# A group-normed convolution and a five-step matching pursuit on one core: the hand-written order of work of all engines is replaced by another

## The reference

```python
x = x + conv3x3_circular(_gn(x), L0_conv_weight)          # 64 -> 64 channels
x = x + pursuit(_gn(x), L1_conv_dictionary)

def pursuit(z, dictionary):        # patches of 64 x 4 x 4 = 1024 numbers, 16384 in all
    D = dictionary / norm          # (1024, 512)
    h_bar = (D.T @ X).T; h = h_bar; G = D.T @ D + 1e-5 * I
    for k in range(1, 6):
        index = argmax(|h| where not yet chosen)
        L = cholesky row from G[I, index];  x_stack = solve with L, h_bar[I]
        h = h_bar - x_stack @ G[I]
    return D @ coeffs
```

## Time and profile before

| what | value |
|---|---|
| device time, median of 3 runs | 3638.73 us (3585.6 to 3663.25) |
| profiled execution | 3610.05 us, its span 3608.2 us |
| mean granted TensorE clock | 0.916 |
| busy: PE, DVE, ACT, POOL | 85%, 71%, 65%, 53% |
| bytes moved by DMA | 428.38 MB, 119 GB/s |
| the chain that ended last | PE 51%, issue 11%, POOL 11%, ACT 11%, DVE 9%, DMA 5% |

### The profile page before, as it was taken

How to read it: one execution, slowest core, us unless ns; L and a number is a source line. 1 busy time by engine, 2 the same in 40 slices (tenths; PEclk the granted TensorE clock), 3 DMA queues, 4 the chain that set the end, 5 groups by cost and what they waited for, 6 DMA issues and landing times.

```text
span 3608.2 us, 35041 instructions
## 1 busy us (share of the span) xinstructions
PE 3072.9 (85%) x9488; PEld 1309.0 (36%) x9488; DVE 2577.4 (71%) x6596; ACT 2361.3 (65%) x3795; POOL 1915.2 (53%) x1861
## 2 busy tenths in 40 slices
PE   6796979889898999989898998989898998985446
PEld 2232334333333434333343433433343433332123
DVE  2027877768787787778777786878778786878871
ACT  3436676667867676667767676776767666665444
POOL 0015565555556565655556565665556566565651
PEclk8998989999999999989999999999999999998768
DMA  3424343533545253444535354344525443342222
GB/s 113 152 88 135 112 146 74 165 92 129 150 130 152 70 189 90 143 120 131 151 93 168 83 170 104 132 132 143 145 72 182 96 157 99 107 113 59 57 61 47
DMA packets 131028, 428.38 MB, mean 119 GB/s; under 512 B 55696, under 2 KB 55952, under 8 KB 106128
## 3 DMA queue, kind: packets, MB, share of 16 engines
q0 software_dynamic: 91136, 202.10, 23.7%
q1 hardware_dynamic: 39696, 224.05, 17.1%
HBM read 289.70 MB, written 136.31 MB: 118 GB/s over the span
## 4 chain that ended last, share of the span: by engine, by line
PE 51%; issue 11%; POOL 11%; ACT 11%; DVE 9%; DMA 5%; ACTq 0%; POOLq 0%; DVEq 0%
PE gen_ps L917 18%; PE gen_ps L908 17%; PE conv_ps L951 10%; POOL v L478 9%; PE conv_ps L958 4%; DMA u<-marked_rows,chosen 3%; ACT hot L542 3%; DVE u L831 2%; ACT score L616 2%; DVE idx L731 2%; DVE top L722 2%; POOL u L490 1%; DVE h L839 1%; ACT rb L554 1%; ACT hot L545 1%
## 5 line engine op out<-in xcount | busy, mean ns | idle before, releaser
L478 POOL DMA_INDIRECT v<-gram_rows,cell x1280 | 1288.4, 1007 | 1009.2 <-DVE cell L740 467.4
L908 PE MATMUL gen_ps<-ct,dt 128*128 128x512 f32 x2048 | 959.1, 624 | 54.3 <-ACT rb L554 36.3
L917 PE MATMUL gen_ps<-dn,z 128*128 128x512 f32 x2048 | 920.6, 603 | 45.9 <-ACT h L577 23.1
L490 POOL DMA_INDIRECT u<-marked_rows,chosen x504 | 552.3, 1096 | 511.3 <-DVE chosen L736 216.4
L951 PE MATMUL conv_ps<-xh,wc 128*128 128x512 f32 x1536 | 727.7, 625 | 76.1 <-ACT xa L584 75.1
L616 ACT ACTIVATE score<-h 128x512 f32<-128x512 f32 x640 | 380.0, 605 | 383.1 <-DVE h L839 250.1
L908 PEld LDWEIGHTS gen_ps<-ct,dt 128*128 128x128 f32 x2048 | 400.8, 200 | 568.9 <-issue 546.7
L917 PEld LDWEIGHTS gen_ps<-dn,z 128*128 128x128 f32 x2048 | 388.2, 193 | 535.3 <-issue 497.2
L722 DVE MAX8 top<-score 128x8 f32<-128x512 f32 x640 | 417.2, 690 | 212.0 <-ACT score L616 197.0
L831 DVE SCALAR_TENSOR_TENSOR u<-u,nl 128x512 f32<-128x512 f32 x748 | 515.6, 748 | 72.7 <-DMA u<-marked_rows,chosen 69.7
L951 PEld LDWEIGHTS conv_ps<-xh,wc 128*128 128x128 f32 x1536 | 301.8, 200 | 470.5 <-issue 469.3
(11 more groups left out here) (103 smaller groups left out, 1860.2 us busy)
## 6 DMA issues: line engine op xcount, KB each, us to landing
xh<-x_paired SPq DMA_DIRECT2D x128, 650.0 KB, 4.0
xa<-x_pairs SPq DMA_DIRECT2D x64, 1024.0 KB, 6.8
y_rows<-xa SPq DMA_DIRECT2D x64, 1024.0 KB, 5.1
y_rows<-rb POOLq DMA_DIRECT2D x64, 1024.0 KB, 8.5
v<-gram_rows,cell POOLq DMA_INDIRECT x1280, 2.4
u<-marked_rows,chosen POOLq DMA_INDIRECT x504, 3.9
...
```

Source lines behind the costliest of these rows:

```text
L478: pool.indirect_dma_start(v[:, g, k - 1, j, t:t + 1], None, cells, bass.IndirectOffsetOnAxis(ap=cell[:, g, k // (KMAX - 1), j, t:t + 1], a ...
L490: pool.indirect_dma_start(kept(img, g, k, t), None, marked, bass.IndirectOffsetOnAxis(ap=chosen[:, g, t:t + 1], axis=0))\
L908: last = pe.matmul(to[:], dt_[:, a, d, :], ct[:, a, :], start=(a == 0), stop=(a == NA - 1))
L917: last = pe.matmul(to[:], z[:, t % 2, d // PATCH, d % PATCH, :], dn[:, d, :], start=(d == 0), stop=(d == ND - 1))
```

## The change

No instruction is added, removed or resized. Another table stands in each of the plans (`VECTOR_PLAN`, `SCALAR_PLAN`, `ADD_PLAN`, `BANKS`, and the tail's vector, scalar and add plans), and PE's calls in `period` and `tail` stand in another order. In the changed file lines are one higher in this part (L616 becomes L617).

Of the diff, one or two lines of each plan, the new `BANKS`, and PE's period from convolve 1 on:

```diff
...
 VECTOR_PLAN = {
-    1.5: [("co", 0)], 5: [("ce", 0, 0)], 8.5: [("ce", 0, 1)], 23.5: [("co", 1), ("ce", 1, 0)], 29.5: [("gn", 1, 1)],
+    1.5: [("co", 0)], 3: [("ce", 0, 0)], 10.5: [("ce", 0, 1)], 23.5: [("co", 1)], 24: [("ce", 1, 0)],
+    30: [("ce", 1, 1), ("gn", 1, 1)], 31: [("gn", 1, 2), ("gn", 1, 3)], 37: [("gn", 0, 1)],
...
 SCALAR_PLAN = {
-    39: [("re", 1, 7), ("rt", 0), ("h", 2), ("h", 3)],
...
+    0: [("z", 4), ("oh", 0, 0, 1)],
+    37: [("h", 2), ("re", 1, 6)], 39: [("rt", 0), ("h", 3), ("re", 1, 7)],
...
 ADD_PLAN = {
-    4: [(0, 0)], 6: [(0, 1)], 7: [(1, 0)], 8: [(1, 1)],
+    4: [(0, 0)], 5: [(0, 1)], 7: [(1, 0)], 9: [(1, 1)],
 }
...
 BANKS = (
-    (("corr", 4), ("corr", 7), ("re", 0, 2), ("re", 0, 5), ("re", 1, 0), ("re", 1, 3), ("re", 1, 5), ("re", 1, 7)),
-    (("corr", 5), ("re", 0, 0), ("re", 0, 3), ("re", 0, 6), ("re", 1, 1), ("corr", 0), ("corr", 1), ("corr", 2)),
-    (("corr", 6), ("re", 0, 1), ("re", 0, 4), ("re", 0, 7), ("re", 1, 2), ("re", 1, 4), ("re", 1, 6), ("corr", 3)),
+    (("corr", 4), ("corr", 7), ("re", 0, 2), ("re", 0, 5), ("re", 1, 0), ("corr", 0), ("re", 1, 4), ("re", 1, 6)),
+    (("corr", 5), ("re", 0, 0), ("re", 0, 3), ("re", 0, 6), ("re", 1, 1), ("re", 1, 3), ("re", 1, 5), ("corr", 3)),
+    (("corr", 6), ("re", 0, 1), ("re", 0, 4), ("re", 0, 7), ("re", 1, 2), ("corr", 1), ("corr", 2), ("re", 1, 7)),
 )
...
                     convolve(i, 1)
                 if p:
                     turn(i - 2, 0, 0)
+                if own:
+                    convolve(i, 2)
+                if p:
+                    turn(i - 2, 0, 1)
+                if own:
+                    convolve(i, 3)
                 if b:
                     correlate(i, 1, 5)
-                if p:
-                    turn(i - 2, 0, 1)
-                if own:
-                    convolve(i, 2)
-                    convolve(i, 3)
+                if own:
+                    convolve(i, 4)
                 if b:
                     correlate(i, 1, 6)
                 if p:
                     turn(i - 2, 0, 2)
                 if own:
-                    convolve(i, 4)
+                    convolve(i, 5)
                 if p:
                     turn(i - 2, 0, 3)
                 if b:
...
                 if p:
                     recon(i, 2, 0, 0)
                     recon(i, 2, 0, 1)
-                    recon(i, 2, 0, 2)
-                if own:
-                    convolve(i, 5)
-                if p:
-                    recon(i, 2, 0, 3)
                 if own:
                     convolve(i, 6)
                 if p:
+                    recon(i, 2, 0, 2)
+                    recon(i, 2, 0, 3)
                     recon(i, 2, 0, 4)
+                if own:
+                    convolve(i, 7)
+                if p:
                     recon(i, 2, 0, 5)
                     recon(i, 2, 0, 6)
-                if own:
-                    convolve(i, 7)
-                if p:
+                    recon(i, 2, 0, 7)
                     turn(i - 2, 1, 0)
-                    recon(i, 2, 0, 7)
+                    turn(i - 2, 1, 1)
                 if own:
                     average(i, 1)
-                if p:
-                    turn(i - 2, 1, 1)
-                if own:
-                    spread(i, 1)
                 if p:
                     turn(i - 2, 1, 2)
                     turn(i - 2, 1, 3)
+                if own:
+                    spread(i, 1)
+                if p:
                     recon(i, 2, 1, 0)
                     recon(i, 2, 1, 1)
                     recon(i, 2, 1, 2)
+                if own:
+                    correlate(i, 0, 0)
+                if here[-1]:
+                    average(i + 1, 0)
+                if p:
                     recon(i, 2, 1, 3)
                 if own:
-                    correlate(i, 0, 0)
+                    correlate(i, 0, 1)
                 if p:
                     recon(i, 2, 1, 4)
                     recon(i, 2, 1, 5)
                 if own:
-                    correlate(i, 0, 1)
-                if here[-1]:
-                    average(i + 1, 0)
+                    correlate(i, 0, 2)
                 if p:
                     recon(i, 2, 1, 6)
                 if here[-1]:
                     spread(i + 1, 0)
+                if own:
+                    correlate(i, 0, 3)
                 if p:
                     recon(i, 2, 1, 7)
-                if own:
-                    correlate(i, 0, 2)
                 if here[-1]:
                     bias(i + 1, 1 - par)
-                if own:
-                    correlate(i, 0, 3)
...
```

26 lines of the change are left out of this document (12 added, 14 removed), and 107 rows, old and new, of tables (SCALAR_PLAN, TAIL_SCALAR_PLAN, TAIL_VECTOR_PLAN, VECTOR_PLAN).

## The result

| | median | lowest to highest | runs |
|---|---|---|---|
| before | 3617.81 us | 3585.60 to 3663.25 | 19 |
| after | 3584.13 us | 3577.72 to 3589.55 | 19 |

The ratio of the times is 0.9934, with a 95% interval of 0.9911 to 0.9957: 0.7% faster, within the 2% called the same. That ratio is taken from the runs that count as fast alone; the medians of the table, over all runs, would give 0.9907. The forecast was 3627 us as against a median of 3638.73, a ratio of 0.9968. The spreads say more than the medians: 78 us before, 12 us after, and the fastest run before takes what every run takes after. The profiled execution after took 3581.48 us (span 3579.5), the one before 3610.05.

A forecast was written before the change was run, and what follows sets the result against it. TensorE, 85% busy, was bounded by two chains of waits setting its 204.6 us period. From 3610.05, 13 x 0.3 added, 10 (start) and 6 (tail) subtracted gave 3598; carried to the median, 3627 us, range 3530 to 3700.

The forecast's parts named there:

- The even case: Steady period: convolve 3's hole moves to convolve 4, later delays are repaid; total as summed, 3627 us, chance 0.63.
- The step: PE between convolve 4 and the turns: runs through without gaps, each evacuation there in time, the last with 1.8 us to spare.
- the 0.5 us charged for the add: First add lands about +130, `re` (0, 4) would start at +129.5: 0.5 us charged, making the period 204.9.
- The first MAX8: DVE at the start of a period's pursuit: a sign of being right was this MAX8 split by 3 to 4 us.
- Start: Second period: correlate's 13.42 us wait for `h` 0 is relieved by new buffers and earlier statistics; 10 us gain taken.
- the lower bound: Gain in the second period from below: the DVE work behind holds it anyway, gain 0.
- Tail: Last image: `ce` (0, 1) moves under the gathers, less the late score and perhaps 2 elsewhere; net gain 6, bounds -4 to 14.
- the gain of 8: Last image: `ce` (0, 1), 8.1 us, moves behind the pick, under gathers for which DVE idled 21.93 us; gain 8.
- the 4 us charged for the late score: Start of the tail: the seam's late score costs +4, set against the gain there.
- Case 2: Scores and `hot` rows come 3.6 us earlier than placed: 6.4 us a period, 83 us, 3540 us; chance 0.21.
- chain A: From the last correlate's end over the pursuit on DVE and ACT to convolve 3; one of two chains said to set the period.
- Case 3: Pursuit stays late, prepared `hot` rows don't repay it: recon (1, 0) 5.5 us later, 72 us, 3695 us; chance 0.16.

The follow-up runs named there:

- the experiment: Changed kernel with the three tail plans and the order in `tail` taken back: 3594.27 us, 10.4 us slower than the changed kernel.
- another: The changed kernel, unedited, measured again on chip B against the kernel before: 3583.89 us, ratio 0.9841.
- made to happen by hand: Changed kernel with evacuation 3 and `z` 7 earlier on ACT: 3571.63 us on chip B, 12 us less than the changed kernel.

## Why the prediction was right, and where not

Against T = 1595.66 (the end of the last correlate), the ninth period came out as placed by hand:

| | forecast | after |
|---|---|---|
| convolve 0 | +4.8 | +4.3 |
| the four MAX8 end | +11.5 | +11.3 |
| `ce` (0, 0) ends, pick | +24.2, +24.7 | +24.0, +24.5 |
| convolve 4 starts, ends | +57.0, +67.8 | +56.4, +66.1 |
| copy of recon (0, 2) | +110.4 | +110.1 |
| `ce` (1, 0) ends | +117.9 | +118.4 |
| last `ce` ends | +148.0 | +148.8 |
| recon (1, 0) starts | +150.0 | +150.7 |
| period | 204.9 | 204.9 |

**The even case** holds: the steady period is what it was. The wait before convolve 4 is 2.82 us (3.6 placed), none stands before correlate 5, the average's wait of 10.12 us is gone, as is the one of correlate (1, 1).

**Missed: `z` 7.** "PE then runs through: correlate 6, convolve 5, correlate 7" failed at correlate 7 by 2.40 us. The step named evacuations only. It left out that ACT's `z` 7 stands behind scores that DVE paces, and that DVE would wait 5.11 us for rows `u` because the earlier evacuation 3 lets the stores start in the middle of their gathers. That the sum still met the period to 0.1 us is luck in part. The wait before convolve 4 was 0.8 us shorter than placed and its clock cost 1.7 us, not 2.8; with the 2.40 us of `z` 7 recon (1, 0) started 0.7 us late; and the 0.5 us charged for the add were not lost.

**Mis-described, without effect.** The first MAX8 is not split: `co` (0) and the norm's steps come first, DVE reaches it at +8.4, and the scores come just ahead of each MAX8 from there. The first add was charged 0.5 us. In the ninth period PE has no gap before or behind recon (0, 4); the adds' landing is 7.9 to 10.1 us there, median 8.0. The estimate of 4.4 us by the Trainium skill's formula (page "DMA: Bandwidth & Descriptors", section "Anatomy of one DMA — SWDGE (gpsimd) path") stays off by a factor of 1.8, and nothing hangs on it.

**Start.** 10 us forecast, 9.0 in period 1 and 3.2 ahead of it: the term was right in size. The wait moved, as the lower bound feared, but only in part: average (1, 1) waits 14.37 us there and correlates (1, 0) and (1, 2) 6.06 and 3.67.

**Tail.** 6 forecast, 9.1 in the profiles and 10.4 in the experiment: the gain of 8 was nearly right (7.2 us of the wait), and the 4 us charged for the late score don't show.

**Not foreseen: the long periods.** The prediction took one ordinary period for all of them, although 3 of the 13 from period 2 to 14 were long in the trace it read, and it said: "I cannot tell which level a new median takes". The starts of convolve 0 would have told: what the long ones exceed the others by is 22.6 us in that run alone, and with up to 10 us each, some eight of them make the spread of 78 us (an estimate; only one undisturbed profile of the kernel before shows them). They are the part of the 28.7 us that start and tail do not explain, and, as far as one profile can say, the likely reason why the ratio came out at 0.9934 in one series and 0.9841 in another. The forecast took 12 us off the profiled run and the profile after takes off 28.7: 10 of the 17 us between them are these periods, for which the sum had no term. So the time landed in the range with about a third of the gain left out of the sum.

**The rivals.** Case 2 (chain A closes by itself) did not happen; made to happen by hand it gives 12 us, not 83, since the gathers' chain takes its place 57 us later. Case 3 did not happen: the `hot` rows in advance are made, and the last `ce` waits for ACT at its last three rows only, by 0.34, 0.62 and 1.10 us.
